# A state space layer with two states side by side on the partition halves

## The chip, the cores and the metric

The kernel runs on one core of a Trainium2 chip. What is measured is the device time of one execution in microseconds (us), from the first to the last work on the core; lower is better. The engines are called PE (TensorE; PEld is its weight load), DVE (VectorE), ACT (ScalarE), POOL (GpSimd) and SP (SyncE, which here only starts transfers). Each takes its own instructions strictly in the order in which they are written, and waits where a semaphore has not reached a value.

## The reference

A decoder of two layers on x of shape 4 x 1024 x 256, all float32. Only its first part is edited, a state space layer with 512 inner channels and 16 states per channel:

```
xc, z = split(layernorm(x) @ W_in)            # 512 channels each
xc    = silu(causal_conv(xc, 4 taps) + conv_b)
dt_r, Bm, Cm = split(xc @ W_xproj)            # 16, 16 and 16 columns
dt    = softplus(dt_r @ W_dt + b_dt)          # step sizes, one per token and channel
A     = -exp(A_log)                           # channel x state
for each token t, channel e, state n:
    h[e,n] = h[e,n] * exp(dt[t,e] * A[e,n]) + dt[t,e] * xc[t,e] * Bm[t,n]
    y[t,e] = sum over n of h[e,n] * Cm[t,n]
y     = (y + xc * D) * silu(z)
x     = x + y @ W_out
```

The recurrence starts from zero in each of the four sequences. Cross attention, a routed feed-forward layer, self attention, a second cross attention and a second routed layer follow.

## The kernel before

The 4096 tokens are taken in 8 chunks (`NCH`) of 512 tokens (`CH`); two chunks make a sequence, so an even chunk starts from zero and an odd one from the states that the even one left. The channels lie on the partitions, in 4 blocks of 128 (`ME`, index m). The states go in 8 pairs (`PAIRS`, index j). An item is one pair of states for one block of channels in one chunk: 32 items a chunk (`ITEMS`, index s inside a chunk), 256 in all (index G). Its tiles `pD`, `drive` and `hc` are 128 x 2 x 512, where the middle index k is the state of the pair, and exist three times (`RINGS`).

For an item
- ACT makes the decays (`decay`, L580 to L598): one exponential per state, of `dt` times a column of `a_neg`, into the PSUM tile `pD`. In even chunks it also writes a zero into the first column of the second state (L596).
- POOL makes the drives (`drives`, L532): `dtx` (which is dt times xc) times the B rows, 128 x 1024 in one instruction.
- DVE runs the recurrence (`scans`, L432). In even chunks one scan over both states, 1024 long, is enough: the zero decay in the middle starts the second state afresh (L439). In odd chunks each state has a scan of 512, which starts from its column of `carried` (L445).
- DVE multiplies with the C rows (`weigh`, L448), into `hc`.
- PE adds up over the states (`state_sum`, L845): two products with a 128 x 128 identity into `pY`, of one bank, after a product with the diagonal `skip` at j = 0. After eight items DVE takes `pY` out and gates it (`finish`, L458), at s = 1, 9 (11 in chunk 0), 17 and 25.
- In even chunks ACT keeps the last states of each item (`keep`, L575).

Everything for the next chunk is woven in by a hand-written order of the same s on every engine. ACT handles the decays of item s + 2 at its step s, with readings of PSUM between their halves (`read_of`) and further work behind them (`more_of`): Silu of the inner channels at s = 21, the step sizes of the next chunk at s = 25 to 28 with their logarithms at s = 26 (L673), each change between Silu, logarithm and exponential with a table load. PE makes the projections in the bank `pA`, which goes from use to use in the order `ORDER`. POOL finishes the step sizes (`step_sizes`, L363 to L376): four instructions of 128 x 512, of which the second waits for the logarithm, the third gives dt and the fourth dtx. They stand ahead of the drive of s = 3, 9 and 15 (blocks 1 to 3 of this chunk) and of s = 31 (block 0 of the next one). At s = 18 POOL also normalises 512 rows for a later chunk.

SP writes the B and C rows of a chunk to DRAM (L333) and loads them back, broadcast to all 128 partitions, pair by pair (L339, L342), each as soon as its buffer is free. Behind them stands a transfer of 4 MB that blanks a part of a table for a later stage (`fill_rows`).

## Time and profile before

| | |
|---|---|
| median of three runs | 3156.37 us (3152.83 to 3161.01) |
| the profiled execution | 3155.42 us |
| its span from first to last instruction | 3153.9 us |
| busy over the span: PE, DVE, ACT, POOL | 2825.9, 2063.7, 1471.9, 1510.8 us |
| granted TensorE clock, mean over the span | 0.956 of full speed |

Busy shares over the span mix stages of different kinds. The state space layer is the part up to about 1019 us; there POOL's drives (597.2 us), PE's sums (501.6 us), the scans (292.8 us in even and 313.8 us in odd chunks), the weighing (308.1 us) and the decays are the costliest groups. Of the chain that ended last, the page names only the last stage, so the layer has to be read from its own windows, waits and timelines. A row of a timeline gives start, duration, engine, line, operation, output and inputs, the count of instructions merged, and in brackets the idle time before it with the engine and line that ended it.

### The profile page before, as it was taken

How to read it: one execution, taken by the hardware profiler on the slowest of the kernel's cores; microseconds unless marked ns; L12 is line 12 of the kernel's file. 1: busy time of each engine (PE TensorE's matmuls, PEld its weight loads, DVE VectorE, ACT ScalarE, POOL GpSimd, SP SyncE). 2: the span in 40 equal slices, each digit the busy share in tenths (PEclk: the TensorE clock that was granted, in tenths of full speed). 3: DMA queues.
4: the chain of work that ended last, by engine and by line, in shares of the span. 5: the costliest groups of instructions: out<-in, count | busy, mean ns of one | idle time of the engine just before them, and what ended most of it. 6: DMA issues, size and time to landing. Idle time of an engine off the chain costs nothing. (4 is left out here: it accounts for less than half of the span.)

```text
span 3153.9 us, 41299 instructions
## 1 busy us (share of the span) xinstructions
PE 2825.9 (90%) x14210; PEld 1841.1 (58%) x14210; DVE 2063.7 (65%) x3705; ACT 1471.9 (47%) x2768; POOL 1510.8 (48%) x1192
## 2 busy tenths in 40 slices
PE   6898988988986877899999999988878999999998
PEld 2343343433432664555556555556657888888887
DVE  7899999999999744577777777658862222222221
ACT  5667666676763400366666666645531111111111
POOL 5788787888886544133433343256751111111111
PEclk8999999999999878999999999989988999999999
DMA  7135044053150054213232222211116665566662
GB/s 237 48 114 162 21 143 144 18 162 121 41 172 0 28 166 150 82 32 82 60 88 58 67 59 59 65 44 35 51 66 211 203 190 184 184 189 202 205 189 61
DMA packets 283854, 346.31 MB, mean 110 GB/s; under 512 B 85787, under 2 KB 238551, under 8 KB 283591
## 3 DMA queue, kind: packets, MB, share of 16 engines
q1 hardware_dynamic: 260399, 310.17, 31.8%
q0 software_dynamic: 16704, 27.21, 3.7%
q10 hardware_dynamic: 6544, 6.30, 0.7%
q8 instruction: 115, 1.88, 0.2%
q14 instruction: 92, 0.75, 0.1%
HBM read 234.69 MB, written 107.95 MB: 109 GB/s over the span
## 5 line engine op out<-in xcount | busy, mean ns | idle before, releaser
L542 POOL TENSOR_TENSOR mb_drive<-mb_dtx,mb_b_rep 128x1024 f32<-128x1024 f32 x255 | 597.2, 2358 | 181.9 <-DVE mb_pD L439 89.0
L853 PE MATMUL mb_pY<-mb_hc,ident 128*128 128x512 f32 x1024 | 501.6, 615 | 57.1 <-DVE mb_hc L456 56.8
L1986 DVE TENSOR_REDUCE at_nm_of<-at_pS 128x2 f32<-128x256 f32 (+1 forms) x630 | 383.3, 635 | 113.0 <-PE at_pS L1976 57.4
L3161 POOL DMA_INDIRECT out<-et_y,et_to x71 | 112.0, 1577 | 661.0 <-DVE et_y L3215 406.7
L3205 DVE TENSOR_TENSOR et_mT<-et_silu,et_pU 128x512 f32<-128x512 f32 (+1 forms) x160 | 100.2, 627 | 470.7 <-ACT et_silu L3176 470.7
L3176 ACT ACTIVATE et_silu<-et_pG 128x512 f32<-128x512 f32 (+1 forms) x160 | 87.9, 549 | 652.6 <-PE et_pU L3237 652.6
L853 PEld LDWEIGHTS mb_pY<-mb_hc,ident 128*128 128x128 f32 x1024 | 189.7, 194 | 328.7 <-issue 184.4
L598 ACT ACTIVATE mb_pD<-mb_dt,mb_a_neg 128x512 f32<-128x512 f32 x384 | 259.6, 688 | 154.6 <-DVE mb_hc L456 143.0
L439 DVE TENSOR_TENSOR_SCAN mb_pD<-mb_pD,mb_drive 128x1024 f32<-128x1024 f32 x128 | 292.8, 2288 | 43.0 <-ACT mb_pD L596 40.5
L445 DVE TENSOR_TENSOR_SCAN mb_pD<-mb_pD,mb_carried,mb_drive 128x512 f32<-128x512 f32 x256 | 313.8, 1269 | 8.0 <-ACT mb_pD L598 8.0
L456 DVE TENSOR_TENSOR mb_hc<-mb_pD,mb_c_rep 128x1024 f32<-128x1024 f32 x256 | 308.1, 1204 | 1.0 <-PE mb_pY L853 1.0
L1973 PE MATMUL at_pS<-at_kT,at_qT 128*128 128x128 f32 (+1 forms) x757 | 273.2, 382 | 24.7 <-DVE at_nm_of L1986 15.5
L2060 ACT ACTIVATE at_e<-at_pE 128x512 f32<-128x512 f32 x384 | 218.6, 598 | 135.2 <-PE at_pE L2049 131.3
L3237 PE MATMUL et_pG<-et_hT,t_wg 128*128 128x256 f32 (+1 forms) x1280 | 273.6, 357 | 0.5 <-ACT et_hT L3171 0.5
L3237 PE MATMUL et_pU<-et_hT,t_wu 128*128 128x256 f32 (+1 forms) x1280 | 273.2, 357 | 0.0
L2049 PE MATMUL at_pE<-at_qT,at_kT 128*128 128x512 f32 (+3 forms) x768 | 268.6, 392 | 2.5 <-DMA at_qT<-at_nmT 1.1
L3248 PE MATMUL et_pO<-t_wd,et_mT 128*128 128x256 f32 x1136 | 268.3, 382 | 1.1 <-DVE et_mT L3205 1.1
L2067 POOL TENSOR_SCALAR_AFFINE_SELECT at_v_rows<-at_v_rows 128x256 f32<-128x256 f32 x96 | 58.7, 628 | 387.5 <-ACT at_v_rows L2060 387.5
L3237 PEld LDWEIGHTS et_pG<-et_hT,t_wg 128*128 128x128 f32 x1280 | 226.7, 192 | 27.8 <-ACT et_hT L3171 0.9
L3237 PEld LDWEIGHTS et_pU<-et_hT,t_wu 128*128 128x128 f32 x1280 | 224.4, 191 | 25.6
L3248 PEld LDWEIGHTS et_pO<-t_wd,et_mT 128*128 128x128 f32 x1136 | 208.8, 190 | 26.2 <-DVE et_mT L3205 1.2
L1973 PEld LDWEIGHTS at_pS<-at_kT,at_qT 128*128 128x128 f32 x757 | 146.3, 194 | 56.3 <-DVE at_nm_of L1986 33.6
(491 smaller groups left out, 4986.2 us busy)
## 6 DMA issues: line engine op xcount, KB each, us to landing
t_wg<-in_t_wgT SPq DMA_DIRECT2D x40, 1024.0 KB, 6.1
t_wu<-in_t_wuT SPq DMA_DIRECT2D x40, 1024.0 KB, 9.0
t_wd<-in_t_wdT SPq DMA_DIRECT2D x40, 1024.0 KB, 11.3
mb_b_rep<-mb_rows SPq DMA_DIRECT2D x64, 512.0 KB, 5.6
mb_c_rep<-mb_rows SPq DMA_DIRECT2D x64, 512.0 KB, 4.9
t_h_sorted<-blank SPq DMA_DIRECT2D x6, 4160.0 KB, 19.9
t_h_sorted<-blank SPq DMA_DIRECT2D x18, 1170.0 KB, 6.3
t_h_sorted<-blank SPq DMA_DIRECT2D x12, 1040.0 KB, 5.8
```

Of the source, the lines that this page charges most:

```text
L439: nc.vector.tensor_tensor_scan(both(pD), both(pD), both(drive), 0.0, ALU.mult, ALU.add).then_inc(s_scan, 2)
L445: nc.vector.tensor_tensor_scan(pD[r][:, k, :], pD[r][:, k, :], drive[r][:, k, :], carried[:, m, 2 * j + k:2 * j + k + 1], ALU.mult, ALU.ad ...
L456: nc.vector.tensor_tensor(hc[r][:, :, :], pD[r][:, :, :], c_rep[:, 2 * j:2 * j + 2, :], ALU.mult).then_inc(s_hc, 1)
L542: nc.gpsimd.tensor_tensor(drive[G % RINGS][:, :, :], dtx[:, m, :].unsqueeze(1).to_broadcast([P, 2, CH]), b_rep[:, 2 * j:2 * j + 2, :], ALU ...
L598: nc.scalar.activation(pD[r][:, k, :], dt[:, m, :], ACT.Exp, scale=scale).then_inc(s_dec, 1)
L853: last = nc.tensor.matmul(pY[:, :], K.ident[:, :], hc[G % RINGS][:, k, :], start=False, stop=(j == PAIRS - 1 and k == 1))
L1973: last = nc.tensor.matmul(out[:, x * w:(x + 1) * w], qT[b][:, a, h, qb * P:(qb + 1) * P], kT[b][:, a, h, w0:w1], start=True, stop=not diag)
L1986: nc.vector.tensor_reduce(nm_of[t % 2][:, w0 // 512, sides[0]:sides[0] + m, qb], score_bank(t, k)[:, 0:m * w].rearrange("p (a w) -> p a w" ...
L2049: last = nc.tensor.matmul(pE[a][:, at:at + w], kT[b][:, a, h, kb * P:(kb + 1) * P], qT[b][:, a, h, q0:q0 + w], start=(n == 0), stop=n == l ...
L2060: nc.scalar.activation(e[g % NE][:, a, :], pE[a][:, :], ACT.Exp).then_inc(s_ex, 1)
L3237: last = nc.tensor.matmul(out[:, x, 0:w * P], weights[:, k, col:col + P], hT[q][:, k, 0:w * P], start=(k == 0), stop=(k == KD - 1))
L3248: last = nc.tensor.matmul(pO[q][:, a, :], mT[j][:, x, a * P:(a + 1) * P], wd[i % 3][:, j * PAIR + x, :], start=(j == 0 and x == 0 and a == ...
```

## The change

The two states of a pair lie on the two halves of the partitions, and the middle index k is now the half of the channel block. Partition h*64 + p of `drive[:, k, :]` is state 2j + h of channel k*64 + p.

- dt and dtx are needed in that layout too: each half of the channels on both partition halves. They are copied from SBUF to SBUF by eight transfers per block and chunk (`twins`), into `dt2` and `dtx2`, which exist three times (`TWINS`). SP issues them for m = 0 between the B and C rows of j = 2 and j = 3, for m = 1 and 2 behind those of j = 7, and for m = 3 behind `fill_rows`.
- B and C rows are loaded to 64 partitions each, two transfers per pair where one was, and with half the bytes in all.
- As both halves of the free index have the same state, one scan of 1024 serves in odd chunks too. It starts from `carried[..., 0:1]`. For the second half, ACT writes the zero decay as in even chunks and adds exp(dt[0]*A) times the carried state to the first element of the second half's drive; these factors are made once per block (`opening`).
- The sum over states folds the partition halves: two products with a 128 x 64 matrix `fold`, into the partitions 0 to 63 and 64 to 127 of `pY`; the product with `skip` is cut the same way.
- POOL makes the step sizes of block 0 ahead of the drive of s = 29 and no longer of s = 31.
- `A_log` comes in the new layout from the host.

```diff
+    HP = P // 2
+    TWINS = 3
...
-        a_neg = sb("a_neg", [P, ME, NST])
+        a_neg = sb("a_neg", [P, ME, 2, PAIRS])
+        fold = sb("fold", [P, HP])
...
-        b_rep, c_rep = sb("b_rep", [P, NST, CH]), sb("c_rep", [P, NST, CH])
+        dt2, dtx2 = sb("dt2", [P, TWINS, 2, CH]), sb("dtx2", [P, TWINS, 2, CH])
+        b_rep, c_rep = sb("b_rep", [P, PAIRS, CH]), sb("c_rep", [P, PAIRS, CH])
...
-        carried = sb("carried", [P, ME, NST])
+        carried = sb("carried", [P, ME, PAIRS, 2])
+        opening = sb("opening", [P, ME, PAIRS])
...
+            def twins(ch, m):
+                nth = ch * ME + m
+                q = nth % TWINS
+                for made, to, s_made, s_to, s_used, per in ((dt, dt2, s_dt, s_dt2, s_dec, 2), (dtx, dtx2, s_dtx, s_dtx2, s_drv, 1)):
+                    eng.wait_ge(s_made, nth + 1)
+                    if nth >= TWINS:
+                        eng.wait_ge(s_used, (nth - TWINS + 1) * PAIRS * per)
+                    for k in range(2):
+                        for h in range(2):
+                            eng.dma_start(to[h * HP:(h + 1) * HP, q, k, :], made[k * HP:(k + 1) * HP, m, :]).then_inc(s_to[q], 16)
...
-                    eng.dma_start(b_rep[:, 2 * j:2 * j + 2, :], rows_dram[ch % 2][2 * j:2 * j + 2, :].partition_broadcast(P)).then_inc(s_b[j], 16)
+                    for h in range(2):
+                        eng.dma_start(b_rep[h * HP:(h + 1) * HP, j, :], rows_dram[ch % 2][2 * j + h, :].partition_broadcast(HP)).then_inc(s_b[j], 16)
...
+                    if j == 2:
+                        twins(ch, 0)
+                twins(ch, 1)
+                twins(ch, 2)
                 fill_rows(K, eng, K.h1_sorted, ch, NCH, s_fill)
+                twins(ch, 3)
...
+        def drive_of(unit, ch, m, j, r):
+            return unit.tensor_tensor(drive[r][:, :, :], dtx2[:, (ch * ME + m) % TWINS, :, :],
+                                      b_rep[:, j, :].unsqueeze(1).to_broadcast([P, 2, CH]), ALU.mult)
...
             def scans(G):
...
-                for k in range(2):
-                    eng.wait_ge(s_dec, 2 * G + k + 1)
-                    nc.vector.tensor_tensor_scan(pD[r][:, k, :], pD[r][:, k, :], drive[r][:, k, :],
-                                                 carried[:, m, 2 * j + k:2 * j + k + 1], ALU.mult, ALU.add).then_inc(s_scan, 1)
+                eng.wait_ge(s_dec, 2 * G + 2)
+                both = lambda T: T[r][:, :, :].rearrange("p k t -> p (k t)")
+                before = carried[:, m, j, 0:1] if ch % 2 else 0.0
+                nc.vector.tensor_tensor_scan(both(pD), both(pD), both(drive), before, ALU.mult, ALU.add).then_inc(s_scan, 2)
...
+            nc.vector.tensor_tensor(fold[:, :], K.ident[:, 0:HP], K.ident[:, HP:P], ALU.add).then_inc(s_fold, 1)
...
-                    if s == 31 and ch + 1 < NCH:
+                    if s == 29 and ch + 1 < NCH:
                         step_sizes(eng, nc.gpsimd, ch + 1, 0)
...
             def decay(G, k):
...
+                if k == 0:
+                    nc.scalar.activation(pD[r][:, 0, :], step, ACT.Exp, scale=scale).then_inc(s_dec, 1)
+                    if j == 0 and ch % 2:
+                        nc.scalar.activation(opening[:, m, :], a_neg[:, m, 1, :], ACT.Exp,
+                                             scale=dt2[:, (ch * ME + m) % TWINS, 1, 0:1]).then_inc(s_opening, 1)
+                    return
+                nc.scalar.activation(pD[r][:, 1, 1:], step[:, 1:], ACT.Exp, scale=scale)
+                blank = nc.scalar.copy(pD[r][:, 1, 0:1], zeros[:, 0:1])
+                if ch % 2 == 0:
+                    blank.then_inc(s_dec, 1)
+                    return
+                eng.wait_ge(s_opening, ch // 2 * ME + m + 1)
+                eng.wait_ge(s_keep, ch // 2 * ITEMS + G % ITEMS + 1)
+                eng.wait_ge(s_drv, G + 1)
+                nc.scalar.activation(drive[r][:, 1, 0:1], opening[:, m, j:j + 1], ACT.Identity, scale=carried[:, m, j, 1:2],
+                                     bias=drive[r][:, 1, 0:1]).then_inc(s_dec, 1)
...
             def magnitude(ch, m):
                 eng.wait_ge(s_A, use(f"DT{m}", ch))
                 if ch > 0:
-                    eng.wait_ge(s_drv, (ch - 1) * ITEMS + (m + 1) * PAIRS)
+                    twin_made(eng, s_dt2, (ch - 1) * ME + m)
+                    twin_made(eng, s_dtx2, (ch - 1) * ME + m)
...
             def state_sum(G):
...
-                    nc.tensor.matmul(pY[:, :], skip[:, m, :], xc(ch, m), start=True, stop=False)
+                    for k in range(2):
+                        nc.tensor.matmul(pY[k * HP:(k + 1) * HP, :], skip[:, m, k * HP:(k + 1) * HP], xc(ch, m), start=True, stop=False,
+                                         skip_group_check=True)
                 eng.wait_ge(s_hc, G + 1)
                 for k in range(2):
-                    last = nc.tensor.matmul(pY[:, :], K.ident[:, :], hc[G % RINGS][:, k, :], start=False, stop=(j == PAIRS - 1 and k == 1))
+                    last = nc.tensor.matmul(pY[k * HP:(k + 1) * HP, :], fold[:, :], hc[G % RINGS][:, k, :], start=False, stop=(j == PAIRS - 1),
+                                            skip_group_check=True)
                 last.then_inc(s_y, 1)
```

The first readers of a block's copies are `decay` (j = 0, on ACT), `drives` (j = 0, on POOL) and, for the very first item, `first_drive` on DVE: each now waits for the eight transfers and no longer for dt or dtx themselves. `weigh` reads `c_rep[:, j, :]` broadcast over k, and `keep` writes `carried[:, m, j, :]`.

## Rows read from the trace of the kernel before

**Rows 1.** Windows: chunk 1, chunk 2, whole layer; busy us (instructions), PEclk, DMA share, GB/s.

```profile
169.91:290.35 120.44, 108.07 (x263) 46.10 (x261) 117.24 (x111) 80.75 (x131) 100.78 (x54) 1.00 0.36 106
290.35:411.84 121.49, 109.17 (x259) 47.06 (x259) 112.21 (x77) 85.78 (x187) 100.52 (x54) 0.97 0.36 105
39.77:1019.40 979.63, 852.95 (x1993) 363.29 (x1994) 917.13 (x745) 644.23 (x1228) 793.01 (x415) 0.97 0.34 103
```

**Rows 2.** Waits of DVE in the layer: total us, times, longest us.

```profile
DVE mb_pD L439 <- ACT mb_pD L596: 40.5, 30, 5.3
DVE mb_yz L461 <- PE mb_pY L853: 11.2, 8, 2.7
```

**Rows 3.** Timeline of DVE: an odd chunk's first items, an even chunk's items 24 and 25.

```profile
169.91 2.45 DVE L445 TENSOR_TENSOR_SCAN mb_pD<-mb_pD,mb_carried,mb_drive 128x512 f32<-128x512 f32 x2
...
173.40 2.45 DVE L445 TENSOR_TENSOR_SCAN mb_pD<-mb_pD,mb_carried,mb_drive 128x512 f32<-128x512 f32 x2
...
378.87 2.30 DVE L439 TENSOR_TENSOR_SCAN mb_pD<-mb_pD,mb_drive 128x1024 f32<-128x1024 f32 x1 [2.98 <-ACT mb_pD L596]
...
382.20 2.29 DVE L439 TENSOR_TENSOR_SCAN mb_pD<-mb_pD,mb_drive 128x1024 f32<-128x1024 f32 x1
```

**Rows 4.** DVE at the end of chunk 2: timeline, and its waits from 392 to 412.

```profile
387.32 0.69 DVE L461 TENSOR_TENSOR mb_yz<-mb_yz,mb_pY 128x512 f32<-128x512 f32 x1 [1.72 <-PE mb_pY L853]
...
400.89 2.30 DVE L439 TENSOR_TENSOR_SCAN mb_pD<-mb_pD,mb_drive 128x1024 f32<-128x1024 f32 x1 [2.40 <-ACT mb_pD L596]
...
DVE mb_pD L439 <- ACT mb_pD L596: 3.6, 4, 2.4
```

**Rows 5.** Waits of DVE for ACT in chunk 1.

```profile
DVE mb_pD L445 <- ACT mb_pD L598: 2.2, 2, 1.2
```

**Rows 6.** Groups of instructions: an exponential and the zero that ACT writes.

```profile
L598 ACT ACTIVATE mb_pD<-mb_dt,mb_a_neg 128x512 f32<-128x512 f32 x384 | 259.6, 688 | 154.6 <-DVE mb_hc L456 143.0 <-ACT mb_carried L578 0.4
...
L596 ACT COPY mb_pD<-mb_zeros 128x1 f32<-128x1 f32 x128 | 18.9, 147 | 0.0
```

**Rows 7.** Timeline of PE in later stages: products on column groups, a full-width block.

```profile
1407.42 1.07 PE L2099 MATMUL at_pO<-at_e,at_v 128*32 128x512 f32 x8
1408.51 1.06 PE L1939 MATMUL at_pF<-ident,at_qk_hl 128*128 128x128 f32 x8
...
2109.62 1.08 PE L2993 MATMUL xa_pM<-xa_eT,xa_v 77*32 77x128 f32 x32 [0.27 <-ACT xa_eT L2877]
```

**Rows 8.** PE ahead of `finish` in chunk 2: timeline, and the window from 378 to 382.

```profile
378.13 3.48 PE L824 MATMUL mb_pA<-mb_xc,mb_w_x_sb 128*48 128x512 f32 x4 [3.52 <-ACT mb_xnT L602]
...
385.30 1.98 PE L853 MATMUL mb_pY<-mb_hc,ident 128*128 128x512 f32 x4
...
378.00:382.00 4.00, 3.87 (x5) 0.93 (x6) 3.13 (x2) 2.21 (x7) 0.75 (x1) 0.59 0.00 0
```

**Rows 9.** Timeline of DVE and ACT: start of the layer, and chunk 0.

```profile
37.65 1.23 DVE L429 TENSOR_TENSOR mb_drive<-mb_dtx,mb_b_rep 128x1024 f32<-128x1024 f32 x1
39.77 4.48 DVE L439 TENSOR_TENSOR_SCAN mb_pD<-mb_pD,mb_drive 128x1024 f32<-128x1024 f32 x2 [0.90 <-ACT mb_pD L596]
...
94.31 0.69 ACT L620 ACTIVATE mb_xc<-mb_pA,mb_conv_b_sb 128x512 f32<-128x512 f32 x1 [7.67 <-PE mb_pA L814]
...
95.79 2.30 DVE L439 TENSOR_TENSOR_SCAN mb_pD<-mb_pD,mb_drive 128x1024 f32<-128x1024 f32 x1 [5.33 <-ACT mb_pD L596]
```

**Rows 10.** Timeline of ACT and POOL around the step sizes at the end of chunk 2.

```profile
396.82 1.15 ACT L673 ACTIVATE cr_xn<-mb_dtx 128x512 f32<-128x512 f32 x2
...
397.59 1.27 POOL L369 TENSOR_TENSOR mb_rest<-cr_xn,mb_rest 128x512 f32<-128x512 f32 x1 [0.39 <-ACT cr_xn L673]
...
401.50 4.66 POOL L542 TENSOR_TENSOR mb_drive<-mb_dtx,mb_b_rep 128x1024 f32<-128x1024 f32 x2
```

**Rows 11.** One line's transfers, the B rows: issue in ns, landing in us.

```profile
L339 SPq DMA_DIRECT2D mb_b_rep<-mb_rows x64: 319/431/877, 31.0 to 898.2; - x64
...
DMA to landing us min/median/max: 3.8/5.6/15.3
```

More of the change, by code:

```diff
@@ L288, in mamba @@
             sem(n) for n in ("dec", "drv", "scan", "keep", "hc", "y", "fin", "rows", "fill"))
+        s_dt2, s_dtx2 = [sem(f"dt2_{q}") for q in range(TWINS)], [sem(f"dtx2_{q}") for q in range(TWINS)]
+        s_fold = sem("fold")
+        s_opening = sem("opening")
         s_b = [sem(f"b{j}") for j in range(PAIRS)]
@@ L582, in decay @@
                 r = G % RINGS
-                scale = a_neg[:, m, 2 * j + k:2 * j + k + 1]
+                scale = a_neg[:, m, k, j:j + 1]
+                step = dt2[:, (ch * ME + m) % TWINS, k, :]
                 if k == 0:
                     if j == 0:
-                        eng.wait_ge(s_dt, ch * ME + m + 1)
+                        twin_made(eng, s_dt2, ch * ME + m)
                     if G == RINGS - 1:
@@ L593, in decay @@
                             eng.wait_ge(s_keep, back // 2 * ITEMS + (G - RINGS) % ITEMS + 1)
-                if k == 1 and ch % 2 == 0:
-                    nc.scalar.activation(pD[r][:, 1, 1:], dt[:, m, 1:], ACT.Exp, scale=scale)
-                    nc.scalar.copy(pD[r][:, 1, 0:1], zeros[:, 0:1]).then_inc(s_dec, 1)
-                else:
-                    nc.scalar.activation(pD[r][:, k, :], dt[:, m, :], ACT.Exp, scale=scale).then_inc(s_dec, 1)
+                if k == 0:
[14 more added lines that the diff above has]
+                                     bias=drive[r][:, 1, 0:1]).then_inc(s_dec, 1)
             def transposed(ch, k):
@@ L749, in _ @@
             projected(0)
-            nc.scalar.activation(a_neg[:, :, :], a_neg[:, :, :], ACT.Exp).then_inc(s_a, 1)
+            nc.scalar.activation(a_neg[:, :, :, :], a_neg[:, :, :, :], ACT.Exp).then_inc(s_a, 1)
             for m in range(2):
@@ L871, in _ @@
             eng.wait_ge(s_diag, ME * TAPS + ME)
+            eng.wait_ge(s_fold, 1)
             for i in range(NCH):
@@ L3295, in layout, with twin_rows @@
     same = lambda n: np.ascontiguousarray(np.asarray(inputs[n]))
+    def twin_rows(n):
+        a = np.asarray(inputs[n])
+        a = a.reshape(-1, 2, P // 2, a.shape[1] // 2, 2)
+        return np.ascontiguousarray(np.transpose(a, (4, 2, 0, 1, 3)).reshape(P, -1))
     return {
```

49 lines of the change are left out of this document (24 added, 25 removed).

## The prediction

> **What bounds the kernel now.** I read the window totals first. In a chunk of the state space layer DVE is busy 117.24 of 120.44 us, PE 108, POOL 101, ACT 81 [rows 1]. The layer runs from 39.77 to 1019.4 us, a third of the span; the stages behind it are not edited. The waits of DVE then show what little it loses there: 40.5 us to ACT in even chunks and 11.2 us to PE in `finish` [rows 2]. So each DVE instruction saved is time saved, until ACT, which has room on average, becomes late in its bursts. The timeline of DVE gives the pace: an item takes about 3.32 us in an even chunk (one scan over 1024) and 3.49 us in an odd one (two over 512) [rows 3]. Yet the chunks of both kinds last about the same, 121.5 us (chunk 2, from 290.35 to 411.84) and 120.4 us [rows 1]: the even chunk waits for ACT for 3.0 us at s = 24 [rows 3] and for 3.6 us in four waits at s = 28 to 31 [rows 4]; the odd one, with its slower pace and without `keep`, only 2.2 us in all [rows 5].
>
> **The change part by part**, all against the profiled run's 3155.4 us, which is 1.0 us below the median.
>
> *One scan per item in odd chunks.* 4 chunks x 32 items x 0.17 us [rows 3] = -21.8 us.
>
> *What odd chunks then wait for.* They get the even pace, and ACT gets a 1-element copy per item (0.15 us [rows 6]) and an Identity on one column, which no row shows: at least nothing beyond the copy, at most the 0.69 us of a 512-wide operation [rows 6]; I take 0.2, since it is as wide as the copy. That is the load `keep` and copy make in even chunks. At s = 24 (ACT has five Silu and two table loads behind it) the stall grows from 1.0 [rows 5] towards the even 3.0 [rows 3]; no `keep` is in line, I take +1.0 in the three odd chunks that prepare another. Small stalls behind the logarithms at s = 4: 4 x 0.3. The Identity also makes ACT wait for POOL's drive; at s = 18, where POOL has just normalised and is only just in time, that puts ACT between POOL and the scan: 4 x 0.4. Together +5.8.
>
> *State sums on half the columns.* PE does two 64-column products per item where it did two of 128, in different column groups. The nearest rows: with four column groups, 32 matmuls of 128 columns take 1.08 us, while 8 of the same width without groups take 1.06 us [rows 7]. So groups run side by side, and I take 0.95 us for a sum that took 1.9 [rows 8]; bounds: 1.9 (no overlap) and 0.95. A rule speaks against it: the Trainium skill, page "TensorEngine Tiling (Array Packing)", section "Tiling Modes", says that changing the mode drains TensorE, which here happens twice per item. The trace doesn't bear out a price: a grouped block ends and the next full-width one begins at 1408.51 with no gap [rows 7]. By the rule the sum would be worse by less than the bound of no overlap.
> What PE gives DVE: the `finish` waits at s = 25 arise behind a projection at 0.59 of the clock and two sums (the one at 385.30 is what `finish` at 387.32 needs) [rows 4, 8]; they go, -11.2 [rows 2]. In chunk 0, ACT waits 7.67 us for taps that stand behind a skip product and two sums, and DVE then 5.33 [rows 9]; with these three halved, -3.2. Together -14.4.
>
> *Step sizes on POOL at s = 29 instead of 31.* This is where time is lost. Their second operation waits for ACT's logarithm (runs from 396.82, read at 397.59 [rows 10]), so dt is not ready any earlier; but now the drives for s = 29 and 30, formerly made before it, stand behind it. Chain in chunk 2: 397.59, three operations of about 1.3 us, a drive of 2.35 (half of 4.66), 404.0 us. The scan of s = 29 began at 400.89 [rows 4]. It slides by 3.1; ACT's logarithms come 1.8 us sooner, since two halved sums stood ahead of ACT's projection and step sizes; DVE, without the `finish` wait, comes 1.7 sooner. Counted as waits: DVE arrives at 387.32 + 0.6 - 1.7 + 3 x 3.32 = 396.2 and starts at 404.0 - 1.8 = 402.2, a wait of 6.0 instead of the four that sum to 3.6; the later ones drop out, since POOL needs 2.3 us a drive. +2.4 in four even chunks, +9.6. In odd chunks only 1.2 was waited there [rows 5], the wait becomes 6.5, and as ACT's Identity for item 29 waits for that drive, the rounding and step of DT2 behind it make item 30 late by 0.7: +6.0 less 0.2, three times, +17.4. Behind POOL's drives stand only DVE and, in odd chunks, ACT; PE idles with them.
>
> *The copies (`twins`).* 8 transfers per block of channels on SP, about 0.43 us of issue each and 3.8 to 5.6 us to land for 512 KB [rows 11]; now 128 KB, for which I take 2 us to land (bounds 1 and 5.6) after 3 us of issue. For m = 0 they are made during the stall at s = 29 and first read by ACT at s = 30, some 7 us later; for m = 1 to 3 over 10 us are free. Nothing; without that cover, up to 5 us each. SP has other work behind them: B and C rows for j = 3 to 7 are issued 4 us later and have five items; the blank fill and the loads for the next stage slip by some 30 us with nothing waiting. Bytes: B and C halve (8 to 4 MB a chunk), copies add 4 MB. Waits of `magnitude` move to these copies, long landed.
> At the start nothing covers them. The first scan is at 39.77, and dtx is complete when the first drive starts, 37.65 [rows 9]; the queue still carries B and C rows, so with issue and landing (2 + 2 us) the copy of dtx is there at 42; first drive 1.2, scan at 43.3. POOL's step sizes and drives follow; +3.4 at the fourth scan and on.
>
> *Nothing:* `fold` (one DVE instruction of 0.1 us while it waits for ACT), the other shape of `a_neg`, the broadcast C row in `weigh` (same elements), the eight-wide `opening`.
>
> Sum: -21.8 + 5.8 - 14.4 + 9.6 + 17.4 + 3.4 = 0.0, so 3155.4 on the profiled run's scale and **3156 us** by the median.
>
> **Rivals.**
> *POOL's lead absorbs the earlier step sizes* (faster). For it: the same four operations stand at s = 3, 9 and 15, and no DVE wait for POOL shows outside the start. Against: there they don't wait for ACT. If so, the 27.0 us go: 3129. 0.22.
> *Column groups don't overlap* (slower). One mechanism, in `state_sum`: sums stay at 1.9 us. Then -14.4 is 0: 3171; it makes the kernel slower by more than 0.3% once some 10 of these 14 us are missing. Against it are the rows of the later stages [rows 7]. The Trainium skill, page "TensorE: Matmul & The Clock Gate", Part 3, speaks for overlap (2.38 times for three column tiles); this trace agrees in kind, with 32 small matmuls in 1.08 us. 0.14.
> *PE's clock* (slower). After 3.5 us without work the projection runs at a granted 0.59 and takes 3.48 us for four instructions, where the sum's four of the same width take 1.98 [rows 8]. Halved sums leave PE more often idle, and the stall at s = 29 adds 6 us of idleness before the next chunk's products. If these then run at 1.2 GHz, about two products and a sum are late by 3 us at each of 7 ends: +20, 3176. 0.14.
> *The copies land late* (slower): 3 to 5 us at some of the 31 later blocks, 3167 or more: 0.07.
>
> **How the numbers follow.** Forecast 0.43, own range 3147 to 3165. Runs of before spread by 8 us; 0.3% (9.5 us) is what can be told from no change. Faster: first rival 0.22 and 0.05 of the forecast's edge, 0.27. Slower: 0.35 of the last three, of which some 0.04 stay small, 0.31. Same: 0.42. The range must leave out no more than 0.2: it takes in the no-overlap and the clock case above, and below it stops at half the first rival, 3135 to 3176.
>
> **What would show it.** DVE: one scan per item everywhere, 3.32 us apart; at s = 29 in seven chunks a wait for POOL's drive of about 6 us, in place of the waits for ACT. POOL: its second step-size operation preceded by an idle of 4 us or more waiting for ACT. PE: sums of about 1 us, waits in `finish` gone, busy time of the layer down by about 240 us. ACT: no long wait for copies. The forecast is wrong if DVE shows no wait for POOL at s = 29 (too slow), or if sums still take 1.9 us, or the granted clock in the layer falls well below the 0.97 to 1.00 of now (too fast).

## The result, and the profile after

The changed kernel takes 3172.48 us (median of 5 runs, 3170.29 to 3177.85), the kernel before, in the runs beside it, 3154.92 us (5 runs, 3151.82 to 3161.01): a ratio of 1.0058, 95% interval 1.0046 to 1.0070. It is slower by 18 us. The forecast was no change (3156), so the direction is missed; 3172 lies inside the range of 3135 to 3176.

The last `finish` of the layer starts at 1018.70 us in the trace of before and at 1036.96 us in that of after: +18.26 us, against a profiled span that grows by 17.1 (3153.9 to 3171.0). The difference arises in the layer, and every experiment below is read by this moment too ("last finish"). It is one profiled execution for each kernel, but it leaves out what varies behind the layer, where nothing is edited: from the last finish to the end pass 2135.2 us in before and 2134.0 in after, 2145.8 to 2150.5 in e1 to e4, which ran on another chip, and 2127.9 to 2137.5 in e5 to e11. One of the twelve executions of e9, 5168.63 us long, is left out of its ratio.

Windows of after, in the columns of [rows 1]: chunk 1, chunk 2, and the layer.

```profile
182.30:308.40 126.10, 95.43 (x268) 29.88 (x268) 113.99 (x78) 91.85 (x193) 100.48 (x54) 0.88 0.40 101
308.40:429.60 121.20, 95.11 (x268) 29.87 (x268) 112.07 (x79) 87.30 (x195) 100.59 (x54) 0.88 0.42 106
47.30:1037.60 990.30, 750.34 (x2056) 228.64 (x2057) 902.80 (x617) 692.35 (x1496) 792.25 (x415) 0.85 0.40 101
```

Chunk 1, an odd one, has gone from 120.4 to 126.1 us, though DVE is busy for 3 us less in it; chunk 2, an even one, stays at 121. ACT has 11 us more work in the odd chunk. (Chunks 3 and 5 lose less, 3 and 4 us: measured from `weigh` to `weigh`, chunks 1 to 6 last 120.1, 121.8, 123.1, 121.6, 121.9 and 120.7 us before, and 126.1, 121.2, 126.1, 121.9, 125.9 and 120.9 us after.)

The waits of after, against [rows 2]: total us, times, longest.

```profile
DVE mb_pD L476 <- ACT mb_drive L639: 36.8, 21, 5.9
...
DVE mb_pD L476 <- POOL mb_drive L387: 25.4, 9, 5.4
DVE mb_pD L476 <- ACT mb_pD L632: 21.4, 15, 5.3
```

The line that costs most now did not exist before: DVE waits 36.8 us in 21 places for L639, the one-column operation with which ACT starts the second state of an item in odd chunks. The groups of instructions tell the rest (busy us, mean ns, then the idle time before them and what ended it):

```profile
L476 DVE TENSOR_TENSOR_SCAN mb_pD<-mb_pD,mb_carried,mb_drive 128x1024 f32<-128x1024 f32 x128 | 300.6, 2348 | 38.4 <-ACT mb_drive L639 36.8 <-POOL mb_drive L387 1.6
L476 DVE TENSOR_TENSOR_SCAN mb_pD<-mb_pD,mb_drive 128x1024 f32<-128x1024 f32 x128 | 292.6, 2286 | 45.4 <-POOL mb_drive L387 23.8 <-ACT mb_pD L632 21.4
L491 DVE TENSOR_TENSOR mb_yz<-mb_yz,mb_pY 128x512 f32<-128x512 f32 x32 | 21.6, 675 | 3.2 <-PE mb_pY L898 3.2
...
L639 ACT ACTIVATE mb_drive<-mb_opening,mb_drive,mb_carried 128x1 f32<-128x1 f32 x128 | 49.4, 386 | 21.3 <-POOL mb_drive L387 21.3
```

Four things are to be seen. The single scan of an odd chunk, which reads its start from a column, takes 2348 ns, 62 more than that of an even chunk. ACT's one-column operation takes 386 ns, not the 200 of the prediction. The 21.3 us that ACT idles ahead of it are waits for POOL's drive. And `finish` waits 3.2 us in all where it waited 11.2 [rows 2]: the halved sums did what was forecast. Timeline of PE, sums and a projection at the end of chunk 2:

```profile
401.43 1.08 PE L898 MATMUL mb_pY<-mb_hc,mb_fold 128*64 128x512 f32 x4 [0.34 <-DVE mb_hc L486]
404.75 1.98 PE L898 MATMUL mb_pY<-mb_hc,mb_fold 128*64 128x512 f32 x4 [2.24 <-DVE mb_hc L486]
...
414.12 3.40 PE L842 MATMUL mb_pA<-mb_xnT,cr_mb_w_in_sb 128*128 128x512 f32 x4 [3.50 <-ACT mb_dt L694]
```

A sum is four instructions before and after (two to a product). On half the columns it takes 1.08 us where it took 1.98 [rows 8]; at 404.75, where the granted clock is 0.50, it takes 1.98 again. The granted clock of the layer falls from 0.97 to 0.85. PE's busy time in the layer therefore falls by 103 us (852.95 to 750.34) and not by the 240 that the prediction named: the sums take 335.7 us for 501.6, and the other products some 63 us more than before.

The step sizes at s = 29, timeline of DVE at the end of chunk 2 (against [rows 4]) and of chunk 1:

```profile
413.90 2.30 DVE L476 TENSOR_TENSOR_SCAN mb_pD<-mb_pD,mb_drive 128x1024 f32<-128x1024 f32 x1 [5.44 <-POOL mb_drive L387]
...
290.86 2.36 DVE L476 TENSOR_TENSOR_SCAN mb_pD<-mb_pD,mb_carried,mb_drive 128x1024 f32<-128x1024 f32 x1 [5.88 <-ACT mb_drive L639]
...
294.87 2.36 DVE L476 TENSOR_TENSOR_SCAN mb_pD<-mb_pD,mb_carried,mb_drive 128x1024 f32<-128x1024 f32 x1 [0.54 <-POOL mb_drive L387]
...
299.42 2.36 DVE L476 TENSOR_TENSOR_SCAN mb_pD<-mb_pD,mb_carried,mb_drive 128x1024 f32<-128x1024 f32 x1 [1.08 <-ACT mb_drive L639]
```

A wait of 5.4 us, with one of 0.36 us ahead of it, stands where chunk 2 had four that summed to 3.6 [rows 4]; in the odd chunk it is 5.88 and two more follow. ACT's timeline there shows why they follow:

```profile
286.91 0.14 ACT L632 COPY mb_pD<-mb_zeros 128x1 f32<-128x1 f32 x1
290.34 0.39 ACT L639 ACTIVATE mb_drive<-mb_opening,mb_drive,mb_carried 128x1 f32<-128x1 f32 x1 [3.29 <-POOL mb_drive L387]
290.63 0.61 ACT L705 ACTIVATE mb_rest<-mb_dtx 128x512 f32<-128x512 f32 x1
291.28 0.72 ACT L707 ACTIVATE mb_rest<-mb_rest,mb_minus_one 128x512 f32<-128x512 f32 x1
291.90 0.67 ACT L626 ACTIVATE mb_pD<-mb_dt,mb_a_neg 128x512 f32<-128x512 f32 x1
...
297.63 0.19 ACT L654 COPY mb_u<-mb_halo 128x3 f32<-128x3 f32 x1 [1.79 <-PE mb_pA L842]
```

ACT has item 29's decays ready at 287.05 and then stands 3.29 us in its own queue for POOL's drive. Behind it wait the rounding of block 1's step sizes (L705, L707), item 30's decays and, between these, the reading of block 2's projection. As that reading is late, PE's next projection is late too, and ACT waits for it 1.79 us with item 31's second decay behind: the wait of 1.08.

The start, against [rows 9]: DVE, the last transfers of SP ahead of it, and ACT.

```profile
37.40 0.69 DVE L412 TENSOR_TENSOR mb_dtx<-mb_dt,mb_xc 128x512 f32<-128x512 f32 x1
46.02 1.23 DVE L387 TENSOR_TENSOR mb_drive<-mb_dtx,mb_b_rep 128x1024 f32<-128x1024 f32 x1 [7.92 <-DMA mb_dtx<-mb_dtx]
47.33 2.30 DVE L476 TENSOR_TENSOR_SCAN mb_pD<-mb_pD,mb_drive 128x1024 f32<-128x1024 f32 x1
...
39.13 2.52 SPq L348 DMA_DIRECT2D mb_dt<-mb_dt  x4
41.70 2.52 SPq L348 DMA_DIRECT2D mb_dtx<-mb_dtx  x4
...
43.66 0.69 ACT L626 ACTIVATE mb_pD<-mb_dt,mb_a_neg 128x512 f32<-128x512 f32 x1 [4.83 <-DMA mb_dt<-mb_dt]
```

The first scan has moved from 39.77 to 47.33 us. dt was complete at 37.4, but SP was busy with B and C rows until 39.1 and needs 0.63 us for each of the eight copies; the last of dtx is issued at 44.2 and landed at 46.0.

### The profile page after: what moved, and what is told of

Read it like the earlier page. It is cut to its first block and busy times, and to the rows that moved or that the text cites. A ratio compares the mean times of both kernels' runs of the same rounds, so it can differ in the third digit from the quotient of the medians.

```text
span 3171.0 us, 42154 instructions
## 1 busy us (share of the span) xinstructions
PE 2721.9 (86%) x14274; PEld 1707.5 (54%) x14274; DVE 2051.3 (65%) x3578; ACT 1521.1 (48%) x3040; POOL 1509.3 (48%) x1192
## 5 line engine op out<-in xcount | busy, mean ns | idle before, releaser
L387 POOL TENSOR_TENSOR mb_drive<-mb_dtx,mb_b_rep 128x1024 f32<-128x1024 f32 x255 | 595.9, 2357 | 147.6 <-DVE mb_pD L476 121.5
L898 PE MATMUL mb_pY<-mb_hc,mb_fold 128*64 128x512 f32 x1024 | 335.7, 713 | 114.3 <-DVE mb_hc L486 112.6
L476 DVE TENSOR_TENSOR_SCAN mb_pD<-mb_pD,mb_carried,mb_drive 128x1024 f32<-128x1024 f32 x128 | 300.6, 2348 | 38.4 <-ACT mb_drive L639 36.8
L476 DVE TENSOR_TENSOR_SCAN mb_pD<-mb_pD,mb_drive 128x1024 f32<-128x1024 f32 x128 | 292.6, 2286 | 45.4 <-POOL mb_drive L387 23.8
L898 PEld LDWEIGHTS mb_pY<-mb_hc,mb_fold 128*64 128x64 f32 x1024 | 65.1, 152 | 329.3 <-DVE mb_hc L486 271.7
L626 ACT ACTIVATE mb_pD<-mb_dt,mb_a_neg 128x512 f32<-128x512 f32 x256 | 176.5, 690 | 122.1 <-DVE mb_hc L486 106.0
```

What stands on the lines that cost most here:

```text
L387: return unit.tensor_tensor(drive[r][:, :, :], dtx2[:, (ch * ME + m) % TWINS, :, :], b_rep[:, j, :].unsqueeze(1).to_broadcast([P, 2, CH]), ...
L476: nc.vector.tensor_tensor_scan(both(pD), both(pD), both(drive), before, ALU.mult, ALU.add).then_inc(s_scan, 2)
L626: nc.scalar.activation(pD[r][:, 0, :], step, ACT.Exp, scale=scale).then_inc(s_dec, 1)
L898: last = nc.tensor.matmul(pY[k * HP:(k + 1) * HP, :], fold[:, :], hc[G % RINGS][:, k, :], start=False, stop=(j == PAIRS - 1), skip_group_c ...
```

## The experiments

Each is a small edit of the changed kernel. The ratio is to the kernel before on the same chip, with its 95% interval; two decimals of a microsecond stand for one profiled execution. The last two columns are the lengths of an odd and an even chunk, from the first `weigh` of one chunk to that of the next.

| kernel | ratio | last finish | chunk 3 | chunk 2 |
|---|---|---|---|---|
| before | 1 | 1018.70 | 123.1 | 121.8 |
| after | 1.0058 (1.0046 to 1.0070) | 1036.96 | 126.1 | 121.2 |
| e1, step sizes at s = 31 | 1.0008 (0.9998 to 1.0018) | 1022.72 | 122.8 | 119.8 |
| e2, sums at full width | 1.0126 (1.0107 to 1.0146) | 1055.45 | 129.1 | 123.6 |
| e3, two scans in odd chunks | 1.0027 (1.0017 to 1.0037) | 1031.93 | 123.4 | 122.4 |
| e4, first copies early | 1.0054 (1.0034 to 1.0074) | 1036.41 | 127.4 | 121.2 |
| e5, s = 31 and two scans | 0.9998 (0.9988 to 1.0007) | 1020.45 | 121.5 | 121.0 |
| e6, s = 31 and mixed scans | 0.9999 (0.9987 to 1.0010) | 1020.20 | 121.5 | 120.9 |
| e7, no start column | 1.0000 (0.9988 to 1.0012) | 1023.13 | 121.8 | 121.2 |
| e8, e6 and a short start | 0.9978 (0.9968 to 0.9988) | 1017.52 | 121.5 | 120.9 |
| e9, e8 with s = 30 | 0.9978 (0.9963 to 0.9992) | 1017.69 | 121.5 | 120.9 |
| e10, e8 with full-width sums | 1.0003 (0.9991 to 1.0016) | 1024.75 | 120.0 | 122.3 |
| e11, e8 with two scans | 0.9988 (0.9975 to 1.0002) | 1017.95 | 121.5 | 121.0 |

**Step sizes back at s = 31 (e1).**

```diff
-                    if s == 29 and ch + 1 < NCH:
+                    if s == 31 and ch + 1 < NCH:
```

> The changed kernel with only the place of block 0's step sizes on POOL put back, from ahead of the drive of s = 29 to ahead of that of s = 31. Theory: the drives of s = 29 and 30 are made before the logarithm is ready, as in the kernel before, so the seven waits of 5.4 to 5.9 us at s = 29 shrink to what ACT leaves over (about 3 us in even, 3 to 4 us in odd chunks), the 0.5 and 1.1 us behind them stay or go: 3 to 4 us per boundary, 20 to 27 us in all, 3146 to 3152 us, faster than before by 0 to 0.3%. Rival: the earlier place is needed for the copies; then ACT or POOL waits for the copies of block 0 at the start of each chunk, 3 to 5 us each, and the time stays at 3165 to 3175 us.

The last finish comes 14.2 us earlier, less than the 20 to 27 us expected. The wait for POOL at item 29 is gone, and waits for ACT of 2.4 us (even) and 2.52 us (odd) stand in its place. The waits of 0.54 and 1.1 us behind it in odd chunks stay.

**Sums at full width again (e2).**

```diff
-        fold = sb("fold", [P, HP])
+        fold = sb("fold", [P, 2, P])
...
-                    last = nc.tensor.matmul(pY[k * HP:(k + 1) * HP, :], fold[:, :], hc[G % RINGS][:, k, :], start=False, stop=(j == PAIRS - 1),
-                                            skip_group_check=True)
+                    last = nc.tensor.matmul(pY[:, :], fold[:, k, :], hc[G % RINGS][:, k, :], start=False, stop=(j == PAIRS - 1 and k == 1))
```

> The changed kernel with the state sums and the skip product at full width: two 128 x 128 matrices, each the fold in one half of the columns and zeros in the other, so that PE does 128-column products as before the change. Theory: a sum takes 1.9 us and no longer 1.08, the waits in finish come back (8 to 11 us in all) and ACT's chain ahead of the step sizes starts 1.5 us later at seven places: 3180 to 3192 us, with the granted clock in the layer back from 0.85 to about 0.97. Rival: what the halved sums give is taken back by the lower clock; then this kernel is within 4 us of the changed one, or faster.

18.5 us later than after: the halved sums are the part of the change that pays. Without them the changed kernel is 1.3% slower than the kernel before, and not 0.6%. Waits of `finish` of 1.2 to 1.8 us return in chunks 0 to 5, and in odd ones the items behind ACT's logarithms (s = 6 and 7) wait 1.9 us instead of 0.4. The granted clock of the layer is 0.96 here, which did not make up for it.

**Two scans per item in odd chunks (e3).**

```diff
+                if ch % 2:
+                    for k in range(2):
+                        eng.wait_ge(s_dec, 2 * G + k + 1)
+                        nc.vector.tensor_tensor_scan(pD[r][:, k, :], pD[r][:, k, :], drive[r][:, k, :],
+                                                     carried[:, m, j, k:k + 1], ALU.mult, ALU.add).then_inc(s_scan, 1)
+                    return
...
+                if ch % 2:
+                    nc.scalar.activation(pD[r][:, 1, :], step, ACT.Exp, scale=scale).then_inc(s_dec, 1)
                     return
...
```

ACT then writes neither the zero nor the start column in odd chunks.

> The changed kernel with two scans per item in odd chunks again, each from its own column of carried, so that ACT writes two plain exponentials and neither the zero nor the Identity, and does not wait for POOL's drive. Theory: merging the scans gave DVE only 0.11 us an item (14 us), and ACT's extra work and its wait for the drive took about as much back (s = 24: 3.3 against 1.0 us; s = 29 to 31: 7.5 against 5 to 6; s = 7: 1): this kernel is at 3166 to 3174 us, no different from the changed one. Rival: the merged scan is worth its 14 us or the 22 us forecast; then this kernel is at 3184 to 3194 us.

The last finish is 5.0 us earlier: the single scan, which was to bring 16 us net, costs 5. By the ratios it costs more, 1.0058 against 1.0027, or 10 us; the intervals allow 3 to 17 us, so the sign is safe and the size is not. The result lies between the two that were expected. The timeline of DVE in e3, end of chunk 1:

```profile
290.67 2.47 DVE L476 TENSOR_TENSOR_SCAN mb_pD<-mb_pD,mb_carried,mb_drive 128x512 f32<-128x512 f32 x2 [4.96 <-POOL mb_drive L387]
...
294.16 2.45 DVE L476 TENSOR_TENSOR_SCAN mb_pD<-mb_pD,mb_carried,mb_drive 128x512 f32<-128x512 f32 x2
```

There is the same wait at item 29, for POOL itself, and none behind it; s = 24 waits 0.98 us, as before the change. `finish` waits some 0.65 us again at s = 25.

**The start column taken out (e7).** This leaves out a part of the computation: in odd chunks the second state of each pair starts from zero.

```diff
-                eng.wait_ge(s_opening, ch // 2 * ME + m + 1)
-                eng.wait_ge(s_keep, ch // 2 * ITEMS + G % ITEMS + 1)
-                eng.wait_ge(s_drv, G + 1)
-                nc.scalar.activation(drive[r][:, 1, 0:1], opening[:, m, j:j + 1], ACT.Identity, scale=carried[:, m, j, 1:2],
-                                     bias=drive[r][:, 1, 0:1]).then_inc(s_dec, 1)
+                blank.then_inc(s_dec, 1)
```

> The changed kernel without ScalarE's last operation of each item in odd chunks (the addition of the second state's start to the first column of its drive) and without its waits; the merged scan, the zeroed column of the decay and the eight-column exponential stay. The second state of each pair then starts at zero in odd chunks, which is left out of the computation. Theory A (what odd chunks lose at s=24 is ScalarE's 0.39 us per item and its waits for POOL's drive): the wait at s=24 of odd chunks falls from 3.31 us to about 1.0, odd chunks from 126.1 us to 123 to 124, and the last finish by 6 to 9 us to 1028 to 1031. Rival (the scan with a start column itself, 2348 ns against 2286, and POOL's lead set it): the odd chunks fall by less than 1 us each, the last finish stays above 1034.

13.8 us earlier than after, about twice what was expected. So the single scan without its start column gains 8.8 us (e3 to e7), and the start column costs 13.8 (e7 to after). The 8.8 are net of what e7 keeps of ACT's additions, the zero of each item (0.15 us) and the eight-column `opening` of each block (0.28 us). The waits of DVE in the layer of e7 now end with POOL itself at s = 29. Below them, its timeline at s = 24 of chunk 1 and at items 29 and 30:

```profile
DVE mb_pD L476 <- POOL mb_drive L387: 39.8, 9, 5.4
DVE mb_pD L476 <- ACT mb_pD L632: 30.6, 20, 5.2
```

```profile
264.86 2.36 DVE L476 TENSOR_TENSOR_SCAN mb_pD<-mb_pD,mb_carried,mb_drive 128x1024 f32<-128x1024 f32 x1 [2.67 <-ACT mb_pD L632]
...
288.75 2.36 DVE L476 TENSOR_TENSOR_SCAN mb_pD<-mb_pD,mb_carried,mb_drive 128x1024 f32<-128x1024 f32 x1 [5.38 <-POOL mb_drive L387]
...
292.14 2.35 DVE L476 TENSOR_TENSOR_SCAN mb_pD<-mb_pD,mb_carried,mb_drive 128x1024 f32<-128x1024 f32 x1
```

The wait at s = 24 did not go back to the expected 1.0 us: it is 2.67 without any start column (0.98 with two scans, 3.31 in after). Of the 2.33 us that it grew, 1.69 belong to the single scan. It must have both decays before it begins, where the first of two scans runs while ACT makes the second decay. ACT's timelines show it: the first decay of this item ends at 266.66 us in e3 and the scan begins 0.11 us later; in e7 it ends at 263.37 us, and the scan begins 1.49 us later, behind `opening`, a reading of PSUM, the second decay and the zero. The start column adds 0.64 here, and in chunk 3 (waits of after less those of e7, item by item) 0.42 and 0.28 at s = 7 and 18, 0.34 at s = 28, and 0.50, 0.54 and 1.09 at s = 29 to 31.

**First copies issued earlier (e4).** In chunk 0, the copies of dt go out behind j = 0. Those of dtx are issued from ACT's queue, as soon as dtx is there; the diff leaves these lines out.

```diff
-                    if j == 2:
+                    if j == (2 if ch > 0 else 0):
                         twins(ch, 0)
...
```

> The changed kernel with the very first copies made sooner: in chunk 0, SP issues those of dt behind the B and C rows of j = 0 and no longer behind those of j = 2, and ACT's queue issues those of dtx. Theory: the start's 7.5 us are the issue of 12 small transfers ahead of the copies at 0.62 us each and the eight copies one behind the other: the first scan moves from 47.3 to 43 to 44 us and the end by 3 to 4 us: about 3168 us. Rival: the start of the layer is bound by landing times or by PE's own start, and the scan of item 4 does not move by more than 1 us.

The copies of dt are issued from 37.01 us on in place of 39.13. The last of dtx is issued at 40.5 us in place of 44.2, and the first drive gains only 1.07 us, not the 3 to 4 expected:

```profile
44.95 1.22 DVE L388 TENSOR_TENSOR mb_drive<-mb_dtx,mb_b_rep 128x1024 f32<-128x1024 f32 x1 [7.25 <-DMA mb_dtx<-mb_dtx]
```

So the order of issue is not the main thing that holds the start: from the end of the last issue to the first drive now pass 4.5 us where 1.8 passed. Why the copies land later is not shown; two queues now move them side by side with the B and C rows. The last finish is 0.55 us earlier.

**Both parts undone (e5), and the single scan where ACT isn't late (e6).** e5 is the edits of e1 and e3 together. e6 has one scan per item in m = 0 and 1 of odd chunks and in all of the last; the condition goes ahead of e3's two scans:

```diff
+                if ch % 2 and ch < LAST and m >= 2:
...
```

> Two parts of the change undone together: the step sizes of the next chunk back at s=31, and two scans per item in odd chunks (no start column by ScalarE there). The copies, the halved sums and the merged scans of even chunks stay. Theory A (the losses are the earlier step sizes and ScalarE's extra work in odd chunks, and they add up): the last finish falls by the 14.2 us of the first and the 5.0 us of the second, from 1036.96 to 1017.8, and the ratio to the kernel before is 0.999 to 1.001. Rival (both losses are the same wait seen twice, since each ends in a DVE that waits at the end of an odd chunk): the second brings nothing more once the first is gone, the last finish stays at 1022 to 1023 and the ratio at 1.001.

> Step sizes back at s=31, and in the odd chunks one scan per item only in the channel blocks m=0 and m=1 and in the whole last chunk; m=2 and m=3 of chunks 1, 3 and 5 take two scans, so that ScalarE is not given its extra work where it is already late (the wait at s=24). Theory A (the single scan gains 0.11 us per item wherever ScalarE isn't late): against the kernel with s=31 and two scans everywhere in odd chunks, 80 items of 0.11 us less the waits that the start column brings, so the last finish is 4 to 8 us earlier, at 1010 to 1014, ratio 0.996 to 0.999. Rival (ScalarE's extra work in m=0 and m=1 adds to a backlog which comes out at s=24 all the same): the last finish is where it is with one scan everywhere and s=31, 1021 to 1023.

From e5 to e3 the move to s = 29 costs 11.5 us, from e3 to after the single scan costs 5.0. Together that is 16.5 us and not the 19.2 expected from undoing each alone, so the two losses are in part the same: with s = 31 the single scan costs only 2.3 us (e5 to e1). Undoing both leaves +1.75 at the last finish and a ratio of 1. e6 misses its 4 to 8 us: 80 single scans gain nothing over e5. Chunk 3 is 121.5 us in both; of the 1.8 us that 16 scans save there, 1.4 reappear as a wait of 0.45 at s = 7, 0.65 more in `finish` at s = 25 (1.42 for 0.77) and 0.26 more at the next chunk's first item.

Both show what bounds a chunk's end once s = 29 is undone. Timelines of e5 at the end of chunk 2: POOL, DVE at item 31, ACT, PE; the last row is PE at the same place of the kernel before.

```profile
406.99 2.35 POOL L387 TENSOR_TENSOR mb_drive<-mb_dtx,mb_b_rep 128x1024 f32<-128x1024 f32 x1
412.52 4.68 POOL L387 TENSOR_TENSOR mb_drive<-mb_dtx,mb_b_rep 128x1024 f32<-128x1024 f32 x2 [3.19 <-DMA mb_dtx<-mb_dtx]
...
414.95 2.30 DVE L481 TENSOR_TENSOR_SCAN mb_pD<-mb_pD,mb_drive 128x1024 f32<-128x1024 f32 x1 [1.16 <-POOL mb_drive L387]
...
413.40 0.19 ACT L647 COPY mb_u<-mb_zeros 128x3 f32<-128x3 f32 x1 [1.76 <-PE mb_pA L839]
...
414.65 0.16 ACT L637 COPY mb_pD<-mb_zeros 128x1 f32<-128x1 f32 x1
...
409.64 3.73 PE L839 MATMUL mb_pA<-mb_xnT,cr_mb_w_in_sb 128*128 128x512 f32 x4 [3.63 <-ACT mb_dt L691]
...
404.15 2.78 PE L799 MATMUL mb_pA<-mb_xnT,cr_mb_w_in_sb 128*128 128x512 f32 x4 [3.62 <-ACT mb_dt L651]
```

POOL waits 3.19 us for the copy of dtx. But DVE's wait of 1.16 us isn't for POOL, though the row says so: item 31's drive was done at 409.34. It ends with ACT's decay at 414.81, which stood behind a copy that waited 1.76 us for PE's projection. That projection takes 3.73 us at a granted clock of 0.53; in the kernel before it took 2.78 at 0.69, and ACT waited 0.81 us. So here the lower clock has a price, by an estimate from these rows 0.95 of the 1.16 us.

**A short start (e8).** As e6, and of chunk 0's first block VectorE makes the four copies that stay on their partitions; DMA makes the other four. (The same two lines stand for dtx2 behind dtx.)

```diff
+                            if nth == 0 and h == k:
+                                continue
                             eng.dma_start(to[h * HP:(h + 1) * HP, q, k, :], made[k * HP:(k + 1) * HP, m, :]).then_inc(s_to[q], 16)
...
             step_sizes(eng, nc.vector, 0, 0)
+            for k in range(2):
+                nc.vector.tensor_copy(dt2[k * HP:(k + 1) * HP, 0, k, :], dt[k * HP:(k + 1) * HP, 0, :]).then_inc(s_dt2[0], 16)
...
```

> As the kernel with s=31 and mixed scans, but of chunk 0's first channel block the four of eight copies that stay on their partitions (the lower half for the first set of columns, the upper half for the second) are made by VectorE, which has nothing else to do there, and only the four that change partitions by DMA. Theory A (the start is late by the bytes that the copies move beside the B and C rows): the first weigh is 1.5 to 3 us earlier than in the changed kernel (52.01), at 49.0 to 50.5, and the last finish 1.5 to 3 us ahead of the mixed kernel's. Rival (the latency of a transfer and POOL's chain set it, not the bytes): the first weigh moves by less than 1 us, and the last finish by less than 1 us.

The first drive starts 2.29 us earlier than in after, the first `weigh` at 49.73 (52.01), and the last finish is 2.7 us ahead of e6:

```profile
43.73 1.23 DVE L389 TENSOR_TENSOR mb_drive<-mb_dtx,mb_b_rep 128x1024 f32<-128x1024 f32 x1 [3.42 <-DMA mb_dtx<-mb_dtx]
```

Since half of the copies means half of the issues too, e8 doesn't tell bytes from issue slots; e4 says that the slots alone are worth 1. This kernel beats both others: 0.9978 of before, 7 us. Of these the layer's end shows only 1.2 in the profiled execution. The ratios of e5 to e11 all lie 2 to 6 us below what their last finishes say against before, and the unedited stages behind the layer vary by several us from one profiled execution to the next. Where the rest of the 7 us lies stays open.

**Three variations of e8: s = 30 (e9), full-width sums (e10), two scans in all odd chunks (e11).**

> The kernel with mixed scans and the short start, with the next chunk's step sizes on POOL at s=30 in place of 31. With s=31 POOL waits 3.2 us at the first drive of a chunk for the copy of dtx, and DVE 1.2 to 1.4 us behind it; with s=29 DVE waits 5.4 us at item 29. Theory A (every drive that stands behind the step sizes costs DVE about what it is short of slack, so one drive less than at s=29 is nearly free): the boundary waits are within 1 us of those with s=31 and the last finish within 4 us of 1017.5 on either side, ratio 0.995 to 1.000. Rival (a step: once a drive is behind the logarithm, its scan slides by 3 us as at s=29): a wait for POOL of 3 to 5 us at item 30 in seven chunks, last finish 1022 to 1032, ratio 1.000 to 1.005.

> The kernel with mixed scans, s=31 and the short start, with the state sums at full width again (two products of 128 columns per item, 1.98 us, in place of four of 64, 1.08 us). In the changed kernel that cost 18.5 us at the last finish. Theory A (what the halved sums gain is what the wait in finish and behind ScalarE's projections loses, wherever the step sizes stand): the last finish is 12 to 20 us later, at 1030 to 1037, ratio 1.002 to 1.005. Rival (the boundary takes back what finish gains, since with s=31 the copy of dtx arrives at a fixed time): 4 to 8 us later, at 1021 to 1026, ratio 0.999 to 1.001.

> As the kernel with mixed scans, s=31 and the short start, with two scans per item in all odd chunks. With the long start both forms ended together (last finish 1020.45 and 1020.20). Theory A (the single scan's gain of 0.11 us an item goes into ScalarE's waits): the last finish within 0.7 us of 1017.5 and the ratio within 0.001 of 0.9978. Rival (the last chunk's single scans are worth 1 to 3 us and were hidden by scatter): last finish 1018.5 to 1020.5.

At s = 30 all chunks take what they take at s = 31. POOL's wait for the copy falls from 3.19 us (e5) to 0.85 and gains nothing, which confirms that DVE was not waiting for it:

```profile
410.00 4.67 POOL L389 TENSOR_TENSOR mb_drive<-mb_dtx,mb_b_rep 128x1024 f32<-128x1024 f32 x2 [0.85 <-DMA mb_dtx<-mb_dtx]
```

One drive more stands behind the logarithm; in odd chunks DVE waits 0.24 us for it at s = 30 and waits less at s = 31. So what the move costs is a step between s = 30 and 29.

With the full-width sums e10 ends 7.2 us later, not 12 to 20 as expected and not 18.5 as in e2. The halved sums save 2.9 us in `finish` here (9.1 to 6.2) where they saved 7.6 in the changed kernel, and 3.1 us at s = 6, 7 and 12 where they saved 7.3. And they lose 2.2 us at items 31 and 0 (5.6 to 7.7), behind the slow projection at the chunk's end. The granted clock of the layer is back at 0.97 in e10. Its chunk 0 is 3.8 us longer than that of e8, its even chunks are longer (122.3 for 120.9), and its odd ones 3 and 5 even shorter (120.0 for 121.5).

e11 ends 0.4 us after e8, within the expected bound; its ratio is 0.0010 higher, with intervals that overlap.

## Why the prediction was wrong

The step that failed is **one scan per item in odd chunks** with **what odd chunks then wait for**: forecast -21.8 + 5.8, that is -16.0 us, measured +5.0 (e3 to after). Its mechanism was named in the text; the sizes were wrong, all in one direction, and one wait was missing from it.

- *The scan.* 0.17 us an item was taken from the pace of even chunks [rows 3]. But the scan that starts from a column takes 2348 ns, not 2286; odd items are 3.38 us apart, and the gain is 0.11 x 128 = 14.1 us, less by 7.7.
- *s = 24 and the small stalls.* Forecast +5.8; in after the wait at s = 24 is 3.31 in three chunks (+2.33 each for +1.0), and with s = 7, 18 and the last chunk's waits the sum is +10.5. Missing in the step: a single scan has to wait for the second decay. Without the start column 1.69 of the 2.33 us stay (e7), and 1.38 of these lie between the end of the first decay and the scan. The Identity takes 0.386 us, where 0.2 was chosen between 0.15 and 0.69.
- *The chain at s = 29 to 31.* That ACT's wait for POOL delays item 30 by 0.7 us was in the text, under the step sizes (what stands there in ACT's queue is the rounding of block 1's, not of DT2's); the start column brought some 0.50 + 0.54 + 1.09 in each of three chunks, and that it reaches item 31 by way of PE was not seen. By e3, whose three odd boundaries wait 14.9 us in place of 23.9, 9.0 of the 20.4 us below belong here. With them the step comes to -14.1 + 10.5 + 9.0 = +5.4, near the +5.0 of e3.

*Step sizes at s = 29:* forecast +9.6 in even and +17.4 in odd chunks. Counted as it was forecast, as waits of after against those of before, it is +9.4 (4 chunks; three waits of 5.44 and one of 4.14 with the small ones around them) and +20.4. In even chunks the chain was right to half a microsecond: a wait of 5.44 us where 6.0 was forecast. But this isn't what the move costs: undoing it gives back 14.2 us (e1), or 11.5 with two scans (e5), since DVE, no longer held at item 29, then waits at item 31 and at the next chunk's first one, in e5 some 1.2 us in even and 1.6 to 1.8 in odd chunks, for ACT behind PE's projection. That the copies are hidden for m = 0 held, and more widely than was said: not only "during the stall at s = 29", but at s = 30 and 31 as well, where the text feared up to 5 us (e5, e9).

*Halved sums:* forecast -14.4, by waits -14.5, though not where it was put, and its sum is right by luck: `finish` 8.0 (for 11.2), chunk 0's taps nothing (DVE still waits 5.33 there, [rows 9]), and the rest at the first item of chunk 4 (2.3) and at s = 6, 7 and 12 of even chunks (3.0) with smaller ones. At the taps of chunk 0 the halved skip product and first sum took 1.98 and 1.92 us: PE had been without work for 7.33 us, and the granted clock was 0.50, so that ACT's wait fell only from 7.67 to 7.10 us. Undone alone it is worth 18.5 in the changed kernel, 7.2 in e10. The rule that weighed against it (the Trainium skill, page "TensorEngine Tiling (Array Packing)", section "Tiling Modes") shows no price here. In after, a full-width projection begins where the grouped sum of 1.08 us ends.

```profile
297.52 1.08 PE L898 MATMUL mb_pY<-mb_hc,mb_fold 128*64 128x512 f32 x4
...
298.53 1.98 PE L842 MATMUL mb_pA<-cr_xn,cr_mb_w_in_sb 128*128 128x512 f32 x4
```

The rival that column groups don't overlap falls. It is the groups that halve the time, not the narrower matrix: in the kernel before, four products with only 48 columns and no groups take 1.92 us.

```profile
383.45 1.92 PE L824 MATMUL mb_pA<-mb_xc,mb_w_x_sb 128*48 128x512 f32 x4
```

*The start:* forecast +3.4, measured +7.5. Issue was taken as 0.43 us a copy and takes 0.63; two more transfers of B and C per j delay the queue to 39.1; landing for all eight ends at 46.0 in place of 42.

The terms by waits: -14.1 + 10.5 - 14.5 + 9.4 + 20.4 + 7.5 = +19.2, against 18.3 measured and 0.0 forecast. Missing from the sum as mechanisms were the second decay and the way to item 31 through PE; the misses of 7.7 (scan), 4.7 (ACT's waits), 3.0 (odd boundaries) and 4.1 (start) all have the same sign. Two of them came from taking the price of an operation that no row showed from its nearest, leaner relative.

Of the rivals, *POOL's lead absorbs the earlier step sizes* falls (a wait for its drive of 4.1 to 5.9 us in all seven chunks, in odd ones by way of ACT). *PE's clock* came true in its cause and not in its effect: 0.85 in the layer, projections at 3.40 us. In the changed kernel little of it reaches DVE, at most the 3.2 us in `finish` and a part of the 1.08 at item 31; with s = 31 it shows as some 1 us at the end of a chunk, not the 3 that were feared. *The copies land late* holds at the start alone; later, POOL waits for them with s = 31 (3.19 us) and nothing is lost by it. That 3172 lies inside the range is luck: the rivals that set its upper end are not what happened. Of the signs that the text gave, the wait for POOL at s = 29 and sums of about 1 us came; the pace of odd items (3.38 us) and PE's 240 us did not. The range's lower end of 3135 is not half of the first rival's 27 us, as the text says; that would be 3142 or 3143.

## What to carry to other kernels

When two operations are merged, count what the first of the pair could start without: the merged one waits for the last of all inputs, and where the feeding engine is just in time, that gives back what the merge saves. Here 14.1 us of DVE's pace came to 8.8 us by itself, and to a loss of 5 with a fix-up on another engine. A fix-up that needs a third engine's result makes its own engine stand in its queue, with everything behind it: put it where nothing urgent follows. And a step moved ahead to hide a latency is first judged by whether anything critical waits for it: POOL's 3.2 us for the copy cost nothing, while the move by two items cost 11.5 us.
